# Routed mixtures of a decoder kernel: one-hot columns in chunks, maxima per group, biases ahead of the loop, a shared last combination

## The reference

```
h = layernorm(x)
logits = h @ router                      # 4 experts (l0f) or 8 (l1f, l2f)
l0f: y = (silu(h @ Wg[e]) * (h @ Wv[e])) @ Wp[e]   for the one best expert e
l1f: y = sum over the best 2 of softmax weight * (gelu(h @ W1[e] + b1[e]) @ W2[e] + b2[e])
l2f: the same with sigmoid scores divided by their sum, plus 0.1 * a shared expert for all rows
x = x + y
```

## Time and profile before

| what | value |
|---|---|
| runs before | 2049.91, 2051.55, 2054.63 us; median 2051.55 |
| profiled execution, its own time | 2051.39 us |
| its span on the core | 2049.6 us, 40723 instructions |
| busy: TensorE, VectorE, ScalarE, GpSimd | 1594.0, 1073.7, 706.3, 534.8 us |
| l0f: first to last instruction | 417 to 526.6 us |
| l1f | 895 to 1064.5 us |
| l2f | 1277 to 1454.5 us |

### The profile page before, as it was taken

The page is one execution under the profiler, slowest core; times in us unless marked ns, Lnnn a source line. Parts: engine busy times, 40 slices in busy tenths (PEclk is TensorE's granted clock), DMA queues, the critical chain, the costliest instruction groups (busy, mean ns, idle before and its releaser), DMA issues. The chain is left out here.

```text
span 2049.6 us, 40723 instructions
## 1 busy us (share of the span) xinstructions
PE 1594.0 (78%) x15721; PEld 1154.8 (56%) x15721; DVE 1073.7 (52%) x2645; ACT 706.3 (34%) x1468; POOL 534.8 (26%) x766
## 2 busy tenths in 40 slices
PE   6858667939699995965758778888467977768998
PEld 3636334639567662745745446677363663546775
DVE  5447554453555555664148666622548449464432
ACT  1226313512122222632420146344330431336674
POOL 2243223225100003315730141177205105121000
PEclk8959778959899996977979869799668968978999
DMA  2052221127100005205730340176200000000000
GB/s 67 1 119 64 43 62 32 39 87 266 47 24 24 18 17 119 57 30 174 236 124 0 61 97 28 66 234 208 77 3 0 1 3 0 1 16 1 6 6 11
DMA packets 65505, 126.48 MB, mean 62 GB/s; under 512 B 9589, under 2 KB 43011, under 8 KB 65089
## 3 DMA queue, kind: packets, MB, share of 16 engines
q1 hardware_dynamic: 57378, 111.79, 19.0%
q0 software_dynamic: 6208, 10.52, 1.6%
q10 hardware_dynamic: 1728, 1.57, 0.4%
HBM read 81.95 MB, written 10.55 MB: 45 GB/s over the span
## 5 line engine op out<-in xcount | busy, mean ns | idle before, releaser
L1476 DVE TENSOR_TENSOR l1a_kv<-l1a_bank,l1a_layer 128x512 f32<-128x512 f32 x96 | 61.8, 686 | 87.7 <-PE l1a_bank L1406 87.7
L1406 PE MATMUL l1a_bank<-l1a_layer,l1a_RT 128*128 128x256 f32 x384 | 92.2, 384 | 0.0
L1406 PEld LDWEIGHTS l1a_bank<-l1a_layer,l1a_RT 128*128 128x128 f32 x384 | 74.1, 193 | 31.3 <-issue 23.5
L2615 POOL TENSOR_TENSOR l3a_KE<-l3a_WS,l3a_GQ 128x2048 f32<-128x2048 f32 (+10 forms) x22 | 59.0, 2690 | 123.6 <-ACT l3a_GQ L2877 113.0
L2075 ACT ACTIVATE l1f_a<-l1f_bank,l1f_expert 128x128 f32<-128x128 f32 x156 | 44.8, 367 | 77.5 <-PE l1f_bank L1963 77.5
L2714 PE MATMUL l3a_bank<-l3a_KE,ident 128*128 128x512 f32 (+3 forms) x136 | 60.7, 595 | 13.7 <-POOL l3a_KE L2615 13.7
L140 POOL TENSOR_SCALAR l1x_ln_ve<-l1x_ln_mv 128x4 f32<-128x4 f32 x4 | 0.9, 227 | 255.9 <-DVE l1x_ln_mv L135 255.9
L421 DVE TENSOR_REDUCE l0g_nm<-l0g_first_bank 128x8 f32<-128x1024 f32 x32 | 39.1, 1223 | 50.3 <-PE l0g_first_bank L311 50.3
L2075 ACT ACTIVATE l2f_a<-l2f_bank,l2f_expert 128x128 f32<-128x128 f32 x156 | 44.4, 368 | 60.5 <-PE l2f_bank L1963 60.5
L3479 PEld LDWEIGHTS l3f_bank<-arena,l3f_hT 128*128 128x128 f32 x512 | 58.4, 192 | 11.4 <-ACT l3f_hT L3553 11.4
L3471 PE MATMUL l3f_bank<-l3f_slT,arena 128*128 128x512 f32 x128 | 61.6, 604 | 0.8 <-DVE l3f_slT L3620 0.8
(11 more groups left out here) (740 smaller groups left out, 4379.1 us busy)
## 6 DMA issues: line engine op xcount, KB each, us to landing
l1f_expert<-in_experts_l1f SPq DMA_DIRECT2D x39, 514.0 KB, 4.6
l2f_expert<-in_experts_l2f SPq DMA_DIRECT2D x39, 514.0 KB, 4.5
l0f_expert<-in_experts_l0f SPq DMA_DIRECT2D x19, 768.0 KB, 5.2
l1a_layer<-in_layers_l1a SPq DMA_DIRECT2D x12, 385.0 KB, 3.0
l0x_k_stack<-l0x_k_parts SPq DMA_DIRECT2D x24, 128.0 KB, 3.2
l0g_k_stack<-l0g_k_parts SPq DMA_DIRECT2D x24, 128.0 KB, 2.5
l1x_k_stack<-l1x_k_parts SPq DMA_DIRECT2D x24, 128.0 KB, 3.1
l2x_k_stack<-l2x_k_parts SPq DMA_DIRECT2D x24, 128.0 KB, 3.1
```

Of the source, the lines that this page charges most:

```text
L1406: ins = pe.matmul(bK[i // 2][:, (i % 2) * 2 * D:(i % 2 + 1) * 2 * D], state(g)[:, i * T:(i + 1) * T], layer(u)[:, D:3 * D], start=True, st ...
L1476: ins = dve.tensor_tensor(kv[u % 2][:, 2 * c:2 * c + 2, :], bK[c][:, :].rearrange("p (i d) -> p i d", i=2), bias, ALU.add)
L2615: pool.tensor_tensor(heads(qprod[j % 2][:, 0:below * D].rearrange("p (i c) -> p i c", c=D)), heads(WS[:, j:j + 1, :]).to_broadcast([P, bel ...
```

## The change

- **One-hot columns.** mark is gone. mark_tiles and mark_places make the columns of a chunk of eight with one instruction each: oneT (which tile) and oneP (which lane) by comparison, and oneJ[1] by a product, all operands bf16; ScalarE (lane) makes oneJ[0] from oneT, scaled per partition. ScalarE copies column, starts and numbers to bf16 at the start. invert waits for both halves.
- **Maxima per group.** choose takes a group; group 0 stands between the scaling of groups 2 and 3. Each group's logits have a bank of their own. In l2f ScalarE's sigmoid runs per group too. mask_rows does the rest for all.
- **Bias ahead of the loop.** turn_weights, bias, take_weights and add_bias move ahead of the loop on their engines, weigh ahead of find_rows. bias of group 0 waits for to_row, since it writes the bank that find_rows reads; the first turn of the loop waits for the last addition (X_set). In l2f they stand between the wide groups.
- **l2f's order on TensorE.** count_rows comes ahead of all wide_up.
- **Buffers.** Four results ahead become eight (RESULTS_AHEAD), twelve gathers ahead become nine.
- **Combination.** VectorE combines groups 0 to 2; GpSimd (combine_pool) group 3: a product of 1024 elements, then two additions of 512. SyncE loads the groups in the order 0, 3, 1, 2. l0f is as before here.

```diff
-ROWS_AHEAD = 4
-GATHERS_AHEAD = 12
+RESULTS_AHEAD = 8
+GATHERS_AHEAD = 9
...
         self.oneP = sb("oneP", [T, M, P], BF16)
-        self.oneJ = sb("oneJ", [T, M, 2, NT], BF16)
+        self.oneT = sb("oneT", [T, M, NT], BF16)
+        self.oneJ = sb("oneJ", [T, 2, M, NT], BF16)
...
     def invert(self, pe, c):
         q = self.q
-        pe.wait_ge(q["ones_made"], c + 1)
+        pe.wait_ge(q["numbered"], c + 1)
+        pe.wait_ge(q["laned"], c + 1)
         for m in range(c * CHUNK, (c + 1) * CHUNK):
-            ins = pe.matmul(self.side_bank[:, 300:300 + 2 * self.NT], self.oneP[:, m, :],
-                            self.oneJ[:, m, :, :].rearrange("p a j -> p (a j)"), start=(m == 0), stop=(m == self.M - 1))
+            ins = pe.matmul(self.inverse, self.oneP[:, m, :], self.oneJ[:, :, m, :], start=(m == 0), stop=(m == self.M - 1))
         if c == self.M // CHUNK - 1:
             ins.then_inc(q["inverted"], 1)
...
-            pe.wait_ge(q["xt_ready"], self.NT)
...
         pe.wait_ge(q["wT_ready"], g + 1)
         if g:
             pe.wait_ge(q["X_set"], g)
+        else:
+            pe.wait_ge(q["to_ready"], 1)
...
         self.turn_rows(pe, 3)
         self.router(pe, 2)
         self.router(pe, 3)
+        self.count_rows(pe)
         if self.shared:
             self.wide_up(pe, 0)
             self.wide_up(pe, 1)
-        self.count_rows(pe)
-        if self.shared:
             self.wide_down(pe, 0)
-            self.wide_up(pe, 2)
             self.invert(pe, 0)
             self.invert(pe, 1)
-            self.wide_down(pe, 1)
-            self.wide_up(pe, 3)
+            self.wide_up(pe, 2)
             self.invert(pe, 2)
             self.invert(pe, 3)
+            self.wide_down(pe, 1)
+            self.turn_weights(pe, 0)
+            self.wide_up(pe, 3)
+            self.bias(pe, 0)
+            self.turn_weights(pe, 1)
             self.wide_down(pe, 2)
+            self.bias(pe, 1)
+            self.turn_weights(pe, 2)
             self.wide_down(pe, 3)
+            self.bias(pe, 2)
+            self.turn_weights(pe, 3)
+            self.bias(pe, 3)
         else:
             for c in range(chunks):
                 self.invert(pe, c)
+            if not self.gated:
+                for g in range(NG):
+                    self.turn_weights(pe, g)
+                    self.bias(pe, g)
         pe.wait_ge(self.q["to_ready"], 1)
+        if not self.gated:
+            pe.wait_ge(self.q["X_set"], NG)
         self.turn(pe, 0)
         self.turn(pe, 1)
         for j in range(self.NT):
...
             if j:
                 self.down(pe, j - 1)
         self.down(pe, self.NT - 1)
-        if not self.gated:
-            for g in range(NG):
-                self.turn_weights(pe, g)
-                self.bias(pe, g)
     def take_rows(self, act, g):
...
+    def lane(self, act, c):
+        q, at = self.q, slice(c * CHUNK, (c + 1) * CHUNK)
+        act.wait_ge(q["tiles_marked"], c + 1)
+        act.activation(self.oneJ[:, 0, at, :], self.oneT[:, at, :], ACT.Identity, scale=self.w["lane"]).then_inc(q["laned"], 1)
+
     def scalar(self, act):
         q = self.q
+        chunks = self.M // CHUNK
         act.copy(self.earlier[:, :], self.w["earlier"]).then_inc(q["tables"], 1)
         act.copy(self.blocks[:, :], self.w["blocks"]).then_inc(q["tables"], 1)
+        act.copy(self.column[:, :], self.w["column"])
+        act.copy(self.starts[:, :], self.w["starts"][:, 0:self.NT])
+        act.copy(self.numbers[:, :], self.w["numbers"]).then_inc(q["tables"], 1)
         for g in range(NG):
             self.take_rows(act, g)
+            if self.shared and g:
+                self.squash(act, g - 1)
         if self.shared:
-            act.wait_ge(q["lg_ready"], 1)
-            act.activation(self.sc[:, :, :], self.oh[:, 0:NB, :], ACT.Sigmoid).then_inc(q["sc_ready"], 1)
-            self.wide_activate(act, 0)
-            self.wide_activate(act, 1)
+            self.squash(act, NG - 1)
         act.wait_ge(q["totals_made"], 1)
         act.copy(self.totals[:, :], self.turn_bank[0:self.R, 0:T]).then_inc(q["totals_ready"], 1)
         if self.shared:
+            self.wide_activate(act, 0)
+            self.wide_activate(act, 1)
+            self.lane(act, 0)
+            self.lane(act, 1)
+            self.lane(act, 2)
+            self.lane(act, 3)
             self.wide_activate(act, 2)
+            self.take_weights(act, 0)
             self.wide_activate(act, 3)
-        elif not self.gated:
-            act.wait_ge(q["diff_ready"], 1)
-            act.activation(self.inv[:, :], self.den[:, :], ACT.Exp).then_inc(q["e_ready"], 1)
+            for g in range(1, NG):
+                self.take_weights(act, g)
+        else:
...
-    def choose(self, dve):
+    def choose(self, dve, g):
         q, k = self.q, self.k
-        lg = self.side_bank[:, 0:NB * 8].rearrange("p (i e) -> p i e", i=NB)
-        NR, K, M = self.NR, self.K, self.M
-        dve.wait_ge(q["logits_made"], NG)
+        at = slice(g * GI, (g + 1) * GI)
+        NR = self.NR
+        lg = self.banks[g][:, 0:GI * 8].rearrange("p (i e) -> p i e", i=GI)
+        dve.wait_ge(q["logits_made"], g + 1)
         if self.shared:
-            dve.tensor_tensor(self.oh[:, 0:NB, :], lg, self.w["gate_bias"].unsqueeze(1).to_broadcast([P, NB, 8]), ALU.add)\
+            dve.tensor_tensor(self.lg[:, at, :], lg, self.w["gate_bias"].unsqueeze(1).to_broadcast([P, GI, 8]), ALU.add)\
                .then_inc(q["lg_ready"], 1)
-            k.wait_alone(dve, q["sc_ready"], 1)
+            k.wait_alone(dve, q["sc_ready"], g + 1)
         else:
-            dve.tensor_copy(self.sc[:, :, 0:NR], lg[:, :, 0:NR]).then_inc(q["lg_ready"], 1)
-            k.wait_alone(dve, q["lg_ready"], 1)
-        for i in range(NB):
+            dve.tensor_copy(self.sc[:, at, 0:NR], lg[:, :, 0:NR]).then_inc(q["lg_ready"], 1)
+            k.wait_alone(dve, q["lg_ready"], g + 1)
+        for i in range(g * GI, (g + 1) * GI):
             ins = dve.max(self.mx[:, i, :], self.sc[:, i, :])
         ins.then_inc(q["settled"], 1)
         k.wait_alone(dve, q["settled"], self.step())
-        for i in range(NB):
+        for i in range(g * GI, (g + 1) * GI):
             ins = dve.max_index(self.ix[:, i, :], self.mx[:, i, :], self.sc[:, i, :])
         ins.then_inc(q["settled"], 1)
         k.wait_alone(dve, q["settled"], self.step())
...
         dve.wait_ge(q["settled"], self.step())
-    def mark(self, dve, c):
-
-        w, NT = self.w, self.NT
-        codes = w["codes"].rearrange("p (m a) -> p m a", a=2)
-        for m in range(c * CHUNK, (c + 1) * CHUNK):
-            dve.tensor_scalar(self.oneP[:, m, :], w["column"], self.split[:, 0, m:m + 1], None, ALU.is_equal)
-            ins = dve.scalar_tensor_tensor(out=self.oneJ[:, m, :, :], in0=w["starts"][:, 0:NT].unsqueeze(1).to_broadcast([P, 2, NT]),
-                                           scalar=self.split[:, 1, m:m + 1], in1=codes[:, m, :].unsqueeze(2).to_broadcast([P, 2, NT]),
-                                           op0=ALU.is_equal, op1=ALU.mult)
-        ins.then_inc(self.q["ones_made"], 1)
+    def mark_places(self, dve, c):
+
+        at = slice(c * CHUNK, (c + 1) * CHUNK)
+        dve.tensor_tensor(self.oneP[:, at, :], self.column[:, :].unsqueeze(1).to_broadcast([P, CHUNK, P]),
+                          self.split[:, 0, at].unsqueeze(2).to_broadcast([P, CHUNK, P]), ALU.is_equal)
+
+    def mark_tiles(self, dve, c):
+
+        q, NT = self.q, self.NT
+        at = slice(c * CHUNK, (c + 1) * CHUNK)
+        dve.tensor_tensor(self.oneT[:, at, :], self.starts[:, :].unsqueeze(1).to_broadcast([P, CHUNK, NT]),
+                          self.split[:, 1, at].unsqueeze(2).to_broadcast([P, CHUNK, NT]), ALU.is_equal).then_inc(q["tiles_marked"], 1)
+        self.mark_places(dve, c)
+        dve.wait_ge(q["tiles_marked"], c + 1)
+        dve.tensor_tensor(self.oneJ[:, 1, at, :], self.oneT[:, at, :], self.numbers[:, at].unsqueeze(2).to_broadcast([P, CHUNK, NT]),
+                          ALU.mult).then_inc(q["numbered"], 1)
     def find_rows(self, dve):
...
 ...
-        chunks = self.M // CHUNK
         self.prime_vector(dve)
-        self.norm_vector(dve)
-        self.choose(dve)
+        self.norm_sums(dve, 0)
+        self.norm_sums(dve, 1)
+        self.scale(dve, 0)
+        self.norm_sums(dve, 2)
+        self.scale(dve, 1)
+        self.norm_sums(dve, 3)
+        self.scale(dve, 2)
+        self.choose(dve, 0)
+        self.scale(dve, 3)
+        for g in range(1, NG):
+            self.choose(dve, g)
+        self.mask_rows(dve)
         if self.gated:
             X, Z = self.k.X[:, :, :], self.k.Z[:, :, :]
             dve.tensor_tensor(X, X, Z, ALU.add).then_inc(q["X_set"], 1)
         self.place_rows(dve)
-        for c in range(chunks):
-            self.mark(dve, c)
-            if self.shared and c == 1:
-                self.wide_add(dve, 0)
+        dve.wait_ge(q["tables"], 5)
```

(37 more changed lines are left out.)

85 lines of the change are left out of this document (51 added, 34 removed).

## The result

The changed kernel took 2045.79 us (median of 20 runs, 2040.46 to 2059.62), the kernel before 2052.97 beside it (20 runs): ratio **0.9966**, 95% interval 0.9953 to 0.998, some 7.0 us less where 13.5 were forecast. It is faster, as predicted, but by half as much.

What follows compares the result with a forecast made beforehand. GpSimd's queue was taken to bound l1f's loop, and l2f has the same loop. Savings of 5.0 us (l0f), 5.7 (l1f) and 2.8 (l2f) sum to 13.5, from a median of 2051.55 to 2038 us; range 2026 to 2047.

Steps and rivals of the forecast that it cites:

- Memsets and maxima: VectorE ahead of the loops: memsets -0.4 us per mixture; maxima per group -2.0 in l1f, -1.9 l0f, -1.7 l2f.
- Four chunks: l1f's one-hot columns on VectorE: 7.8 us in place of 13.1, at one element a cycle, -5.3 us.
- two elements a cycle: Rival, one-hot chunks: 0.86 us less a chunk in l1f, 0.7 in l0f, 4.8 less, 2033 us; chance 0.13.
- chunks no faster: Rival, one-hot chunks: step-0 operand costs two cycles an element, 9.3 us more, 2047 us; chance 0.09.
- periods of 3.7 us at 0.50: l1f's bias chain ahead of the loop: 3.7 us a group at granted clock 0.50, 15.8 us in all.
- the stretch from the count: l2f, TensorE's path from counting to first turn (wide groups, inversion, transposes, biases): 41 us.
- clock rival: TensorE: l1f's bias chain at full clock, 2033 us, chance 0.10; l2f's stage at low clock, 2072 us, chance 0.06.
- 4.0 + 6.7 + 4.3 + 0.2: Tails of l1f and l2f: first load, VectorE's 24 instructions, GpSimd's three, handovers, added up to 15.2 us.
- the rival by which they run side by side: Tails: VectorE's and GpSimd's combining do not collide, 11.3 us each, 7.8 us less in all, 2030 us; chance 0.14.
- that last stretch has no idle time: l1f's loop: eight result buffers keep TensorE ahead; 67 steps of 1.325 us, 88.8 us to the last scatter.
- the late first turn: l1f: biases ahead of the loop put the first turn at 945.9 in place of 941.94; last scatter -3.7 us.
- Its 5.0 us: l0f ahead of its loop: 0.4 (memsets) + 1.9 (maxima) + 2.7 (one-hot columns) us saved.

Runs made afterwards that it cites:

- e7: One-hot columns made one by one on f32 as in the kernel before, against the changed kernel; ratio 0.9998 to the kernel before.
- e1: VectorE combines all four groups and GpSimd none, against the changed kernel; ratio 0.9918 to the kernel before.
- e2: GpSimd's group of results loaded first (order 3, 0, 1, 2), against the changed kernel; ratio 0.9961 to the kernel before.
- e10: One small GpSimd memset that nothing needs, late in l1f and l2f, against e6; ratio 0.9822 to the kernel before.
- e11: The changed kernel, unaltered, timed and profiled a second time; ratio 0.9973 to the kernel before.
- e3: Five buffers for expert weights in place of four, against the changed kernel; ratio 0.994 to the kernel before.
- e12: VectorE combines all groups and five expert weight buffers, both against the changed kernel; ratio 0.9899 to the kernel before (second run of this kernel).
- e6: Biases inside the loop, two blocks every fourth tile, against the kernel of e12; ratio 0.9827 to the kernel before.
- e8: Biases behind the loop again as in the kernel before, against e1; ratio 0.9894 to the kernel before.
- e4: Four result buffers and 12 gathers ahead in place of eight and nine, against the changed kernel; ratio 0.9958 to the kernel before.
- e9: 13 gathers ahead in l1f and l2f in place of nine, l0f still nine, against e6; ratio 0.9787 to the kernel before.

## Why the prediction was wrong, and what of it held

The direction was right and the size was not: 13.5 us were forecast and 7.0 measured. Two terms of the sum failed, the two tails and the stretch from first to last scatter. A third part of the shortfall, some 2 us, has no cause shown.

**Ahead of the loops it held.** Memsets and maxima took 2.2 us off l1f and 2.4 off l0f (2.4 and 2.3 forecast), in l2f 1.45 where 2.1 stood. Four chunks took 7.8 us, as forecast: 1024 bf16 elements took 1217 ns, as long as the 1214 of the f32 row that the forecast called one a cycle. Both rivals, two elements a cycle and chunks no faster, fall. The Trainium skill has a finer rule than the table: "Vector Engine (DVE) Microarchitecture Reference", section "5.1 Performance modes — why throughput varies by op and dtype", says that an element read 16 times by a two-source operation on 2-byte operands ran at one a cycle; here it is read 128 times, and the trace agrees. e7 gives the chunks 2.7 us ahead of l0f's loop (the two profiles of the changed kernel, 0.5 and 3.2 us shorter in l0f, can't confirm them in its length), 5.6 to 6.0 in l1f's length and nothing in l2f's.

**The start of the loops held.** l1f's first turn came 50.6 us after the start, exactly as summed with periods of 3.7 us at 0.50. l2f's first scatter came at 68.2, 67.8 forecast; its first turn came 61.5 us after the start where 63.2 were forecast, since the stretch from the count took 38.6 us and not 41, and the first result 5.5 us behind it, not 4.5. Neither clock rival came about.

**Step that failed: the tail.** The sum 4.0 + 6.7 + 4.3 + 0.2 = 15.2 us stood for what measured 3.7 + 10.55 = 14.3 in l1f and 4.0 + 10.55 = 14.5 in l2f, so the collision of VectorE and GpSimd was priced well, and the rival by which they run side by side falls. What it left out is the end of the block: it took the last combining instruction for the end. GpSimd's drain had been hidden behind VectorE since the last scatter; giving GpSimd work behind the scatters uncovered it. From the last scatter to the next layer 18.7 and 18.9 us stood in place of 2.3 + 15.2 = 17.5. As gains, 3.6 us came of the 5.7 forecast, 2.1 too few; the forecast's old tails had left out the 0.3 us to the next layer. That the drain is the cause is shown by e1, e2 and e10.

**Step that failed: "that last stretch has no idle time".** It holds in six of the ten loops named under e11. Four expert buffers let the last weights be issued only when the fourth tile before is through, 6.0 us ahead of that tile's start, near the end, where GpSimd, rid of its gathers, takes results every 1.29 us (why it strikes there is read off the timeline and not tested). It cost 1.3 us a loop in the mean of ten, and 3 in l2f of the first profile. That a fifth buffer removes it is shown by e3, e12 and e6.

**What was never priced.** In l1f the forecast let the late first turn eat most of 7 us, and so it came (3.7 us at the last scatter, forecast and measured). But it never set the move of the biases against leaving them behind the loop: e8 shows that the move loses 7.3 us in l1f's loop and wins 4.9 in its tail.

**l0f.** Its 5.0 us came as forecast, ahead of the loop: the first gather stands 31.1 us after the start, 36.1 before. Its loop spreads. From first gather to last scatter it took 64.5 us before, and 62.9 to 65.7 in the ten profiles that have the changed kernel's l0f (all but e4's and e7's); the whole of l0f took 102.5 to 105.3 us in them, 104.0 in the mean, against 109.4 in the one profile of before. So the 6.9 and 4.2 of the table are two draws from about 5.4.

**What stays open.** The mixtures gave 10.1 and 9.8 us by two profiles, the times 7.0 and some 5.5. Of the 6.5 us between forecast and result the tails account for 2.1 and the late weights for 1.3 a loop; the last 2 or so have no cause shown. The rest of the program took 1591.5 to 1599.4 us in twelve profiled executions (1593.6 in the one of before), so single profiles are not fine enough to place them. Nor does e4 settle what eight results and nine gathers are worth with four weight buffers.

## What to carry over

Work that is given to an idle engine near the end of a block moves that engine's closing drain: look for the end of the drain's own row before a tail is summed by busy instructions. Here GpSimd would have had to be done some 6.4 us ahead of VectorE. Work that is moved out of a tail costs nothing only where it doesn't delay the queue that bounds the loop; the place for it is the slack inside (e8, e6). And where a loop is bound by one queue, count the steps left after its first result: every gather issued while the queue was idle is one less (e9 in l2f; in l1f, where the queue had no gap, it gave nothing).
